# A four-layer cross-attention kernel: one engine meeting taken out between two layers, and the order of issue changed in two earlier places

## The chip, the cores and the metric

The kernel runs on one core of a Trainium2 chip. The time is device microseconds (us) of one launch. The engines are TensorE (PE, matmuls; its weight loads are PEld), VectorE (DVE), ScalarE (ACT), GpSimd (POOL) and SyncE (SP, which here only issues DMAs). Every engine runs its own program in order, and programs wait for each other on semaphores.

## The reference, cut to what matters

Four layers follow one another over `x`, 4 batches of 256 tokens with 256 channels:

```
L0: x = x + tanh(gate) * (softmax(q k^T / 4, masked) v) Wo     16 heads of 16; k, v from layernorm(ctx)
L1: an RWKV block (recurrent scan and channel mixing)
L2: x = layernorm(x + (softmax(q k^T * s + mask) v) Wo + bo)   32 query heads of 8 on 8 key/value heads
L3: twice:  x = x + cross_attention(layernorm(x), ctx)         16 heads of 128, and one extra bias key/value
    then    x = x + gelu(layernorm(x) W1 + b1) W2 + b2
```

All softmaxes subtract the row maximum. The keys and values of L3 come from `ctx` alone, so they are projected early, in the shadow of the layers before.

## The kernel before, in words

There are five stages, written one after the other: `stacked_first` (L0), `rwkv_block` (L1), `stacked_attention` (L2), `wide_stream` (the two attentions of L3) and `mlp`. Between stages the four compute engines meet (`meet`, L294): each drains, signals `arrived`, and waits until SP (`lead`, L300) has cleared all stage semaphores and set each engine's `go`.

**L0 and L2** work in steps (8 each; a step is half of a batch's heads) of 8 slots. In `at`, the number of a slot, negative slots are a run-up. For every head PE first makes the plain scores of a step (`fill`, L636 and L1338), DVE takes row maxima of them, POOL splits these into three bf16 parts, PE turns them (`flip_maxima`), ACT copies the row to SBUF and issues a DMA on its own queue that lays it beside the queries (`fetch_maxima`, L841 and L1541; semaphores `max0_landed`, `max_landed`). Then `transposed_scores` (L648, L1353) gives scores with the maximum already subtracted, ACT takes exponents, `weigh` multiplies by the values. Operands of a step are three-part bf16 rows: they are written to DRAM (`keep_keys0`, `keep_queries0`; `keep_key_parts`, `keep_query_parts`) and read back spread over the partitions (`spread0`, L542: eight DMAs for one step; `spread_rows`, L1238: three DMAs for one batch). SP issues all of these in one written order (`stacked0_sp`, L583; `stacked_sp`, L1291). In L0, `spread0(m)` must have landed before `fill(m, 0)` in slot 8(m-2); step 5 is spread in slot 18, behind `keep_queries0(3)` in slot 17:

```
605:                if prepared(n - 1) is not None and i == 1:
606:                    keep_queries0(sp, prepared(n - 1))
607:                if 1 <= n <= STEPS0 - 4 and i == 2:
608:                    spread0(sp, n + 3)
```

**Units ahead.** The 128 matmul groups that project `ctx` to L3's keys and values (`project_ahead`, L1101: 4 matmuls of 512 columns) are strewn over the slots. The first eight, from a quarter of a value matrix, belong to L0: `first_unit(0)` stands in the opening (L723), the other seven at `FIRST_AT` (L516). In the opening PE turns x and the normalised context of batch 1 (`flip_x(1)`, `flip_a(1)`) and projects keys and queries of batch 1 (L720 to L728); `flip_a(1)` stands behind `first_unit(0)`, which waits for two loads.

**L2's end** (`finish`, L1508): last `weigh`, first query projection of L3 (`project_head`), `flip_od`, DVE `normalise`, `flip_on`, second `project_head`, `project_out` into J1, and `bias_rows_pe` (32 matmuls into bank S0) with ACT's copy of its result to `v17`. SP has meanwhile loaded keys and values of group 0 of L3 in four pieces (`load_kept(sp, 0, 0)`, L1322), issued when the last unit is stored. Then the meeting.

**L3's stream** handles 128 items (8 groups of 16 heads). For item n: `logits(n)` on PE (two matmuls; it waits for its piece in `kept_landed`, for a bias column in `kept_bias`), DVE `maxima`, ACT `exponents`, DVE `divide`, PE `turn`, ACT copy, PE `weigh`, DVE copy, PE `add_head`; `project_query` runs two items ahead. `logits(0)` stands at the start of the stage (L2575), and DVE adds L2's last output to x (L2711, L2713) before `maxima(0)`.

Of the kernel before, what the change touches and what calls it, by code (L numbers as in the profile page):

```python
# [62 lines left out]
def build(nc, d, out):  # L63
    with ExitStack() as ctx:
# [216 lines left out]

        def stage_names():
# [233 lines left out]
        FIRST_AT = [-15, -13, -9, -8, -6, -5, -3]  # L516
# [66 lines left out]
        def stacked0_sp(sp, load_first, load_rest, load_values):  # L583
# [14 lines left out]
            for at in range(-LEAD0, LAST0):  # L598
# [9 lines left out]
                if 1 <= n <= STEPS0 - 4 and i == 2:  # L608
                    spread0(sp, n + 3)
# [5 lines left out]
        def stacked_first():  # L615

            def pe_program(pe):
# [102 lines left out]
                flip_x(1, J0)  # L720
                pe.wait_ge(loaded["ctxT"], 16)
                pe.wait_ge(loaded["quarter"], 16)
                first_unit(0)  # L723
                flip_a(1, O1)
# [3 lines left out]
                queries(1, T1)  # L728
                for at in range(-LEAD0, LAST0):
# [61 lines left out]
                    if at in FIRST_AT:  # L791
                        first_unit(1 + FIRST_AT.index(at))
# [7 lines left out]
            def act_program(act):  # L800
# [69 lines left out]
                fetch_queries(1, T1)  # L870
                act.wait_ge(loaded["const"], 16 * 2)
                act.activation(gate[:, 1:2], gate[:, 0:1], ACT.Tanh).then_inc(gate_ready, 1)
                act.wait_ge(mask_ready, 4)
                for at in range(-LEAD0, LAST0):
                    n, i = at // CHUNKS0, at % CHUNKS0
                    if at - 1 in FIRST_AT:
                        u = 1 + FIRST_AT.index(at - 1)
                        copy_first(act, (J1, O0)[u % 2], u)
# [412 lines left out]
        def stacked_sp(sp, load_wide, load_ahead):  # L1291

            for at in range(IN_TAIL, LAST):
                n, i = at // CHUNKS2, at % CHUNKS2
                b = n // 2
                if i == 0 and n % 2 == 0 and n >= 0 and b + 1 < B:
                    if b > 0:
                        sp.wait_ge(st_done, 4 * b * CHUNKS2)
                    else:
                        sp.wait_ge(filled, SLOTS2 + 1)  # L1300
                    spread_rows(sp, b + 1)
# [7 lines left out]
                if at == 6:  # L1309
                    sp.wait_ge(tail_done, 4)  # L1310
                    load_ahead("k")
# [22 lines left out]
        def stacked_attention():  # L1334
            chunk_order = [(kt, j, gp) for kt in range(TQ) for j in range(2) for gp in range(2)]

            def pe_slots(pe):
# [170 lines left out]
                def finish():  # L1508
# [6 lines left out]
                    flip_od(STEPS2 - 1, T0)  # L1515
                    flip_on(STEPS2 - 1, T1)
                    project_head(pe, 0, 1, 1)
                    project_out(B - 1, J1)
                    bias_rows_pe(pe, 0, S0)
# [7 lines left out]
            def pe_program(pe):  # L1527
                slot, finish = pe_slots(pe)[0:2]
                for at in range(IN_TAIL, LAST):
                    slot(at)  # L1530
                finish()
                meet(pe, "pe")

            def act_slots(act):
# [51 lines left out]
                def finish():  # L1586
# [5 lines left out]
                    bias_rows_act(act, 0, S0)  # L1592
# [7 lines left out]
            def act_program(act):  # L1600
# [4 lines left out]
                meet(act, "act")  # L1605

            def pool_program(pool):
# [49 lines left out]
                meet(pool, "pool")  # L1657
# [109 lines left out]
            def dve_program(dve):  # L1767
# [4 lines left out]
                meet(dve, "dve")  # L1772
# [681 lines left out]
        def load_layer1(split_k):  # L2454
# [22 lines left out]
            "last2_read", "last2_var", "last2_rstd", "last2_normed", "last2_step", "last2_scaled"))  # L2477
        FRONT_AT = 8
        ROWS_AT = 3 * HEADS3 + 12

        def stream_sp(sp, load_wide):

            for n in "qo":
                load_wide(1, n)
# [6 lines left out]
        def wide_stream():  # L2491
# [9 lines left out]
            def pe_program(pe):  # L2501
                def logits(n):
                    g, a, h = of(n)
                    if n >= AHEAD:
# [9 lines left out]
                    mm.then_inc(logits3_done, 1)  # L2514

# [26 lines left out]
                def weigh(n):  # L2542
                    g, a, h = of(n)
                    pe.wait_ge(pt3_ready, n + 1)
                    for st in range(TQ):
# [29 lines left out]
                logits(0)  # L2575
# [65 lines left out]
            def pool_program(pool):  # L2641
                pool.memset(weight_blocks[:, :, :, 16:17], 1.0)
                pool.memset(weight_blocks[:, :, :, 17:32], 0.0)
                for keys, _ in kept:
                    pool.tensor_copy(keys[:, :, S], head_cols("bias_k1")).then_inc(kept_bias, 1)
# [26 lines left out]
            def dve_program(dve):  # L2672
# [193 lines left out]
        def _(sp):  # L2866
# [64 lines left out]
            for i in range(len(programs["pe"]) - 1):  # L2931
# [114 lines left out]
```

## Time and profile before

| | |
|---|---|
| median of 3 runs | 1253.01 us (1250.61 to 1253.26) |
| profiled execution | 1252.52 us; its span 1250.7 us |
| PE busy | 1188.3 us, 95% of the span |
| DVE, ACT, POOL busy | 63%, 43%, 17% |
| granted TensorE clock, mean | 0.984 |

The span is what the trace covers; 1.8 us of the profiled execution lie around it. A granted clock of 1.00 is 2.4 GHz and of 0.50 is 1.2 GHz. Times in the rows are counted from the span's start. The chain that ended last is PE in 86% of the span, so the places of interest are those in which PE stands still or runs at 0.50.

### The profile page before, as it was taken

To read this page: it belongs to the slowest core of one execution; us is meant where nothing else is said; L and a number is where in the kernel's file an instruction comes from. 1 tells how busy PE (TensorE), PEld (TensorE's weight loads), DVE (VectorE), ACT (ScalarE), POOL (GpSimd) and SP (SyncE) were. 2 spreads that over 40 slices of the span, in tenths; PEclk is the share of its full clock that TensorE was granted. 3 is DMA by queue.
4 is the path that set the end of the run, shared out by engine and by line. 5 is a ranking of instruction groups with operands and counts; after the bars stand their busy time and mean duration, and the time that the engine had idled before them with its cause. 6 is when DMAs were issued, how large, how long until landed. Compare 5 with 4: busy or idle time off the path is not lost.

```text
span 1250.7 us, 17685 instructions
## 1 busy us (share of the span) xinstructions
PE 1188.3 (95%) x5936; PEld 837.6 (67%) x5936; DVE 792.5 (63%) x2357; ACT 537.4 (43%) x1233; POOL 216.0 (17%) x430
## 2 busy tenths in 40 slices
PE   6899899999998799999998999999999999999998
PEld 4466554655555344444335888888888888888887
DVE  4655377868685577878754666666656676666530
ACT  2365533445445245455553434343434334343432
POOL 2240152434244101120111000000000000000000
PEclk8998999999999799999999999999999999999999
DMA  8659032021116635154249230302112120500000
GB/s 245 161 159 280 9 129 85 34 76 43 68 48 197 189 144 166 73 164 144 78 146 322 97 130 6 114 23 97 39 55 80 37 99 21 182 1 2 1 9 26
DMA packets 95033, 124.42 MB, mean 99 GB/s; under 512 B 7264, under 2 KB 72960, under 8 KB 92704
## 3 DMA queue, kind: packets, MB, share of 16 engines
q1 hardware_dynamic: 94320, 123.00, 30.4%
q8 instruction: 48, 0.79, 0.3%
q10 hardware_dynamic: 624, 0.30, 0.1%
q14 instruction: 41, 0.34, 0.1%
HBM read 79.33 MB, written 43.65 MB: 98 GB/s over the span
## 4 chain that ended last, share of the span: by engine, by line
PE 86%; DVE 3%; ACT 3%; issue 2%; POOL 2%; DMA 2%; SPq 1%; ACTq 1%; POOLq 0%; DVEq 0%
PE J L2538 9%; PE TT L2546 9%; PE J L2558 9%; PE OO L1112 5%; PE OO L1109 5%; PE TT L2522 5%; PE S L2512 4%; PE OO L2512 4%; PE J L1112 3%; PE J L1376 2%; PE J L323 2%; PE J L1109 2%; PE OO L2779 2%; PE S L1348 2%; PE J L332 2%
## 5 line engine op out<-in xcount | busy, mean ns | idle before, releaser
L2616 ACT ACTIVATE PT<-TT 128x512 f32<-128x512 f32 x128 | 76.4, 597 | 282.4 <-PE TT L2522 282.4
L2651 POOL COPY On<-probs 128x8 f32<-128x8 f32 x128 | 29.2, 228 | 471.3 <-DVE probs L2686 442.1
L2697 DVE TENSOR_SCALAR QK<-J,cols 128x256 f32<-128x256 f32 x126 | 60.9, 484 | 70.3 <-PE J L2538 70.3
L2686 DVE TENSOR_SCALAR probs<-probs,inv 128x257 f32<-128x257 f32 x256 | 79.0, 351 | 4.5
L2522 PE MATMUL TT<-ident,probs 128*128 128x128 f32 x512 | 77.3, 274 | 2.6 <-DVE probs L2686 2.6
L1112 PE MATMUL OO<-ctxT,weights_a 128*128 128x512 f32 x144 | 70.2, 610 | 5.8 <-SPq L307 3.3
L2522 PEld LDWEIGHTS TT<-ident,probs 128*128 128x128 f32 x512 | 64.1, 141 | 16.3 <-DVE probs L2686 3.4
L2692 DVE COPY km<-TT 128x256 f32<-128x256 f32 x128 | 54.2, 423 | 30.8 <-PE TT L2546 30.5
L1109 PE MATMUL OO<-weights_a,ctxT 128*128 128x512 f32 x136 | 69.3, 634 | 3.4 <-SPq L307 2.9
L2402 DVE TENSOR_TENSOR_SCAN early<-km,early 128x256 f32<-128x256 f32 x64 | 64.3, 1044 | 10.9 <-ACT early L2160 10.1
L2546 PE MATMUL TT<-PT,weights_a 128*128 128x256 f32 x256 | 66.2, 381 | 0.0
L2558 PE MATMUL J<-early,km 128*128 128x256 f32 x256 | 65.8, 379 | 0.3 <-DVE km L2692 0.3
L2546 PE MATMUL TT<-PT,early 128*128 128x256 f32 x256 | 65.9, 380 | 0.0
L2558 PE MATMUL J<-weights_a,km 128*128 128x256 f32 x256 | 65.6, 379 | 0.0
L2678 DVE TENSOR_REDUCE maxes<-OO 128x1 f32<-128x257 f32 x128 | 48.5, 420 | 26.0 <-PE OO L2512 25.0
L2678 DVE TENSOR_REDUCE maxes<-S 128x1 f32<-128x257 f32 x128 | 48.4, 420 | 24.8 <-PE S L2512 24.8
L2608 ACT ACTIVATE probs<-S,maxes 128x257 f32<-128x257 f32 x128 | 59.4, 474 | 3.5 <-DVE maxes L2678 3.5
L2608 ACT ACTIVATE probs<-OO,maxes 128x257 f32<-128x257 f32 x128 | 59.3, 473 | 0.1
L2546 PEld LDWEIGHTS TT<-PT,weights_a 128*128 128x128 f32 x256 | 49.2, 192 | 6.9
L2546 PEld LDWEIGHTS TT<-PT,early 128*128 128x128 f32 x256 | 48.5, 190 | 7.0 <-ACT PT L2616 0.4
L2558 PEld LDWEIGHTS J<-early,km 128*128 128x128 f32 x256 | 48.3, 190 | 7.1 <-DVE km L2692 0.5
L2558 PEld LDWEIGHTS J<-weights_a,km 128*128 128x128 f32 x256 | 48.5, 190 | 6.7
(423 smaller groups left out, 2624.2 us busy)
## 6 DMA issues: line engine op xcount, KB each, us to landing
wide_keys<-weights_a SPq DMA_DIRECT2D x43, 256.0 KB, 2.1
wide_values<-weights_a SPq DMA_DIRECT2D x40, 256.0 KB, 2.0
weights_a<-wide_keys SPq DMA_DIRECT2D x16, 512.0 KB, 7.3
weights_a<-wide_values SPq DMA_DIRECT2D x16, 512.0 KB, 8.5
early<-wide_keys SPq DMA_DIRECT2D x16, 512.0 KB, 8.1
early<-wide_values SPq DMA_DIRECT2D x16, 512.0 KB, 9.0
query_parts<-weights_a SPq DMA_DIRECT2D x32, 192.0 KB, 2.7
weights_a<-in_L_xattn_wv SPq DMA_DIRECT2D x2, 2048.0 KB, 8.8
```

The lines of the kernel that those rows point to most:

```text
L1109: mm = pe.matmul(bank_[:, :], ctxT[:, k, b * S + t * P:b * S + (t + 1) * P], values_, start=(k == 0), stop=(k == KC - 1))
L1112: mm = pe.matmul(bank_[:, :], ahead_k[a][:, k, h * P:(h + 1) * P], ctxT[:, k, pair * 512:pair * 512 + 512], start=(k == 0), stop=(k == KC ...
L2402: ins = dve.tensor_tensor_scan(state[j % 2][:, half, 1:S + 1], wT[:, half, :], kv[j % 2][:, half, :], start[:, half, j:j + 1], ALU.mult, A ...
L2512: mm = pe.matmul(L_[n % 2][qt][:, 0:T], QK[:, n % 2, 0, qt * P:(qt + 1) * P], kept[g % 2][0][:, h, :], start=True, stop=True)
L2522: mm = pe.transpose(T0[:, st * S + qt * P:st * S + (qt + 1) * P], P_[n % 2][:, qt, st * P:(st + 1) * P], ident[:, :])
L2538: mm = pe.matmul(J0[:, 0:S], wide[a][0][:, k, h * P:(h + 1) * P], hidden[g % 2][:, k, :], start=(k == 0), stop=(k == KC - 1))
L2546: mm = pe.matmul(T1[:, 0:S], kept[g % 2][1][:, st, h * P:(h + 1) * P], PT[:, n % 2, st * S:(st + 1) * S], start=(st == 0), stop=(st == TQ ...
L2558: pe.matmul(J1[:, qt * S:(qt + 1) * S], avT[:, n % 2, qt * P:(qt + 1) * P], wide[a][1][:, h, :], start=(h == 0 and qt == 0), stop=False)
L2608: ins = act.activation(P_[n % 2][:, qt, 0:T], L_[n % 2][qt][:, 0:T], ACT.Exp, bias=maxes[:, qt, n % 32:n % 32 + 1], accum_out=sums[:, qt, ...
L2616: act.activation(PT[:, n % 2, :], T0[:, :], ACT.Copy).then_inc(pt3_ready, 1)
L2678: ins = dve.tensor_reduce(maxes[:, qt, n % 32:n % 32 + 1], L_[n % 2][qt][:, 0:T], AX_X, ALU.max, negate=True)
L2686: ins = dve.tensor_scalar(P_[n % 2][:, qt, :], P_[n % 2][:, qt, :], inv[:, qt, n % 32:n % 32 + 1], None, ALU.mult)
```

## The change: what it does

Five edits, in order of time.

1. **Opening of L0.** `flip_a(1, O1)` stands ahead of the waits for `ctxT` and `quarter`, so ahead of `first_unit(0)`. `first_unit(1)` stands behind `queries(1, T1)`; six units instead of seven are left for `FIRST_AT`, in other slots. ACT's copies follow.
2. **L0, SP.** `spread0(5)` is issued in slot 16 instead of 18, so ahead of `keep_queries0(3)`.
3. **L2, SP.** The spread of batch 1 waits until the first row of maxima has landed (`max_landed`).
4. **L2, SP, slot 6.** Three more waits, and one instruction that clears the 40 semaphores that stages share by name.
5. **L2 to L3.** No engine meets any more. `logits(0)` is issued between `flip_od` and `flip_on` of L2's end. The bias rows go to bank T1 and wait for `ot2_ready`. The first DVE work of L3 is `maxima(0)` and `divide(0)`; the two additions follow. POOL, SP and PE get single waits in place of the meeting.

```diff
-        FIRST_AT = [-15, -13, -9, -8, -6, -5, -3]
+        FIRST_AT = [-14, -12, -9, -7, -5, -3]
...
-                if 1 <= n <= STEPS0 - 4 and i == 2:
+                if 1 <= n <= STEPS0 - 4 and i == (0 if n == 2 else 2):
                     spread0(sp, n + 3)
...
                 flip_x(1, J0)
+                flip_a(1, O1)
                 pe.wait_ge(loaded["ctxT"], 16)
                 pe.wait_ge(loaded["quarter"], 16)
                 first_unit(0)
-                flip_a(1, O1)
                 pe.wait_ge(keys0_ready, 1)
                 keys(1, T0)
                 pe.wait_ge(queries0_ready, 1)
                 queries(1, T1)
+                first_unit(1)
...
                     else:
                         sp.wait_ge(filled, SLOTS2 + 1)
+                        sp.wait_ge(max_landed, 16)
                     spread_rows(sp, b + 1)
...
                 if at == 6:
                     sp.wait_ge(tail_done, 4)
+                    sp.wait_ge(st_done, 1)
+                    sp.wait_ge(sum_ready, 1)
+                    sp.wait_ge(weighed_ready, 1)
+                    clear_stage(sp, 40)
                     load_ahead("k")
...
                     flip_od(STEPS2 - 1, T0)
+                    logits = slots3["pe"](pe)
+                    logits(0)
                     flip_on(STEPS2 - 1, T1)
                     project_head(pe, 0, 1, 1)
                     project_out(B - 1, J1)
-                    bias_rows_pe(pe, 0, S0)
+                    pe.wait_ge(ot2_ready, STEPS2)
+                    bias_rows_pe(pe, 0, T1)
...
-                meet(pe, "pe")
...
         def stream_sp(sp, load_wide):
 
+            sp.wait_ge(av2_done, 4 * STEPS2)
+            sp.wait_ge(sum_ready, 2 * LAST)
+            sp.wait_ge(max_taken, STEPS2 * SLOTS2)
+            sp.wait_ge(max_landed, 16 * STEPS2)
+            sp.wait_ge(out2_done, B)
             for n in "qo":
                 load_wide(1, n)
...
                 def logits(n):
                     g, a, h = of(n)
+                    if n < AHEAD:
+                        pe.wait_ge(q_ready, n + 1)
+                    if n == 1:
+                        pe.wait_ge(ahead_copied, 2 * UNITS)
...
             def pool_program(pool):
+                pool.wait_ge(av2_done, 4 * STEPS2)
+                pool.wait_ge(ahead_done, 2 * UNITS)
+                pool.tensor_copy(kept[0][0][:, :, S], head_cols("bias_k1")).then_inc(kept_bias, 1)
+                pool.wait_ge(on2_flipped, STEPS2)
                 pool.memset(weight_blocks[:, :, :, 16:17], 1.0)
                 pool.memset(weight_blocks[:, :, :, 17:32], 0.0)
-                for keys, _ in kept:
-                    pool.tensor_copy(keys[:, :, S], head_cols("bias_k1")).then_inc(kept_bias, 1)
+                pool.wait_ge(out2_done, B)
+                pool.tensor_copy(kept[1][0][:, :, S], head_cols("bias_k1")).then_inc(kept_bias, 1)
...
+                maxima(0)
+                divide(0)
+                dve.wait_ge(out2_done, B)
                 dve.tensor_tensor(xn[:, :, :], two(J1), x_of(B - 1), ALU.add).then_inc(last2_read, 1)
                 dve.wait_ge(last2_read, 1)
                 chain.link(dve.tensor_tensor(xn[:, :, :], xn[:, :, :], bo2, ALU.add))
-                maxima(0)
-                divide(0)
...
                 elif i == 2:
                     stacked_sp(sp, load_wide, load_ahead)
-                    lead(sp, 1)
```

The first `weigh` of L3 also waits for `v17_ready`, since it writes bank T1. `copy_first(act, (J1, O0)[1], 1)` stands behind ACT's `fetch_queries(1, T1)`.

## Rows read from the trace of the kernel before

**Rows 1.** Waits on PE: waiting line and releaser; us in total, times, longest
```profile
PE TT L1363 <- DMA weights_a<-early: 4.9, 1, 4.9
```

**Rows 2.** Timeline of the opening: start us, us, engine, line, operands; idle before it
```profile
19.53 0.73 DVE L264 TENSOR_SCALAR xn<-weights_a,moments,rstd 128x256 f32<-128x256 f32 x2 [0.28 <-POOL rstd L271]
20.30 3.75 PE L1109 MATMUL J<-early,ctxT 128*128 128x512 f32 x4 [3.74 <-DMA early<-in_L_xattn_wv]
...
26.11 3.68 PE L323 MATMUL TT<-V,early 128*128 128x256 f32 x8 [1.20 <-ACT V L812]
...
29.63 1.89 PE L323 MATMUL TT<-hT,early 128*128 128x256 f32 x8
```

**Rows 3.** Windows: stretch, length, busy PE PEld DVE ACT POOL, granted clock, DMA
```profile
20.30:29.40 9.10, 7.89 (x16) 4.69 (x17) 1.42 (x4) 1.51 (x3) 0.00 (x0) 0.50 0.72 166
422.10:439.00 16.90, 11.41 (x23) 3.95 (x23) 6.03 (x29) 3.54 (x4) 0.00 (x0) 0.50 0.51 154
674.70:678.00 3.30, 3.30 (x11) 2.73 (x12) 1.10 (x5) 1.51 (x5) 0.07 (x1) 0.50 1.01 421
```

**Rows 4.** Timeline of SP's issues in L0, from 80 us on
```profile
80.85 1.87 SPq L2868 DMA_DIRECT2D early<-in_state  x1
...
86.75 0.90 SPq L539 DMA_DIRECT2D query_parts<-weights_a  x2
...
92.12 0.58 SPq L571 DMA_DIRECT2D km<-query_parts  x1
```

**Rows 5.** Timeline of PE in L0: slots 24, 32 and 48, and step 5's fill
```profile
91.30 0.60 PE L657 MATMUL TT<-early,weights_a 128*128 128x256 bf16 x4
95.97 0.39 PE L643 MATMUL S<-weights_a,km 128*128 128x256 bf16 x1 [4.07 <-DMA km<-query_parts]
...
108.56 0.60 PE L657 MATMUL OO<-km,weights_a 128*128 128x256 bf16 x4
...
129.65 0.60 PE L657 MATMUL TT<-early,weights_a 128*128 128x256 bf16 x4
```

**Rows 6.** Timeline of L2's first slots: spreads, maxima row, a unit, slots 0 and 3
```profile
418.45 0.84 SPq L1245 DMA_DIRECT2D km<-query_parts  x2
...
422.09 0.76 ACTq L1547 DMA_DIRECT2D weights_a<-early  x1
...
424.36 3.78 PE L1109 MATMUL OO<-weights_a,ctxT 128*128 128x512 f32 x4
...
433.08 1.01 PE L1363 MATMUL TT<-weights_a,early 75*128 75x512 bf16 x2 [4.93 <-DMA weights_a<-early]
...
444.74 0.60 PE L1363 MATMUL TT<-weights_a,early 75*128 75x512 bf16 x2
```

**Rows 7.** DMA queues from 426 to 434 us: queue, packets, MB, share
```profile
q10 hardware_dynamic: 51, 0.02, 1.5%
```

**Rows 8.** Line L1161 between 660 and 661.9 us: the first piece's values
```profile
L1161 SPq DMA_DIRECT2D weights_a<-wide_values x1: 508/508/508, 660.9 to 660.9; - x1
...
DMA to landing us min/median/max: 5.1/5.1/5.1
```

**Rows 9.** Timeline from L2's end to the first items of L3
```profile
663.78 0.44 PE L1398 MATMUL TT<-ident,On 128*128 128x128 f32 x2 [0.91 <-DVE On L1707]
...
666.96 1.93 PE L446 MATMUL S<-weights_a,mask_b 128*32 128x256 f32 x32
669.02 0.38 ACT L452 ACTIVATE KT<-S 128x256 f32<-128x256 f32 x1 [4.38 <-PE S L446]
...
670.63 1.10 PE L2512 MATMUL S<-weights_a,QK 128*128 128x257 f32 x4 [1.73 <-POOL early L2645]
670.74 0.69 DVE L2713 TENSOR_TENSOR xn<-xn,rows 128x512 f32<-128x512 f32 x1
...
674.57 1.03 PE L2522 MATMUL TT<-ident,probs 128*128 128x128 f32 x4 [1.97 <-DVE probs L2686]
...
679.34 0.60 PE L2522 MATMUL TT<-ident,probs 128*128 128x128 f32 x4
```

More of the change, by code:

```diff
@@ L280, in build, with clear_stage @@
         shared = []
+        def clear_stage(sp, count):
+            numbers = [s.num for s in shared[:count]]
+            assert numbers == list(range(numbers[0], numbers[0] + count))
+            sp.sem_clear(range(numbers[0], numbers[0] + count))
         def stage_names():
@@ L791, in pe_program @@
                     if at in FIRST_AT:
-                        first_unit(1 + FIRST_AT.index(at))
+                        first_unit(2 + FIRST_AT.index(at))
                 weigh(STEPS0 - 1, 1)
@@ L870, in act_program @@
                 fetch_queries(1, T1)
+                copy_first(act, (J1, O0)[1], 1)
                 act.wait_ge(loaded["const"], 16 * 2)
@@ L876, in act_program @@
                     if at - 1 in FIRST_AT:
-                        u = 1 + FIRST_AT.index(at - 1)
+                        u = 2 + FIRST_AT.index(at - 1)
                         copy_first(act, (J1, O0)[u % 2], u)
@@ L1591, in finish @@
                     act.wait_ge(ahead_stored[2], stores_before(2 * UNITS, 2))
-                    bias_rows_act(act, 0, S0)
+                    bias_rows_act(act, 0, T1)
                 def second_batch():
@@ L1604, in act_program @@
                 finish()
-                meet(act, "act")
             def pool_program(pool):
@@ L1656, in pool_program @@
                 bias_rows_pool(pool, 0)
-                meet(pool, "pool")
             def dve_slots(dve):
@@ L1771, in dve_program @@
                 finish()
-                meet(dve, "dve")
             slots2.update(pe=pe_slots, act=act_slots, dve=dve_slots)
@@ L2477, in build @@
             "last2_read", "last2_var", "last2_rstd", "last2_normed", "last2_step", "last2_scaled"))
+        slots3 = {}
         FRONT_AT = 8
@@ L2499, in of, with first_logits @@
                 return n // HEADS3, n // HEADS3 // B, n % HEADS3
-            def pe_program(pe):
+            def first_logits(pe):
                 def logits(n):
                     g, a, h = of(n)
+                    if n < AHEAD:
+                        pe.wait_ge(q_ready, n + 1)
+                    if n == 1:
+                        pe.wait_ge(ahead_copied, 2 * UNITS)
                     if n >= AHEAD:
@@ L2514, in logits, with pe_program @@
                     mm.then_inc(logits3_done, 1)
+                return logits
+            slots3["pe"] = first_logits
+            def pe_program(pe):
+                logits = first_logits(pe)
                 def turn(n):
@@ L2544, in weigh @@
                     pe.wait_ge(pt3_ready, n + 1)
+                    if n == 0:
+                        pe.wait_ge(v17_ready, 1)
                     for st in range(TQ):
@@ L2573, in add_bias_rows @@
                     mm.then_inc(out3_done, 1)
-                logits(0)
                 for n in range(ITEMS3):
```

## The prediction

> **What bounds the kernel now.** First the page: PE is busy in nearly all of the span, so a reordering can only win where PE stands still or runs at its lower clock. Then the waits of PE, the longest single ones: `transposed_scores` in L2 waits 4.9 us for a DMA that ACT issued [rows 1], and `fill` of step 5 in L0 waits 4.07 us for a spread [rows 5]. Then the timelines around these two, the opening and the layer change, with the windows for the clock. Each standstill is followed by work at 1.2 GHz: the windows behind the opening's wait, around the wait in L2 and at the start of L3 have a granted clock of 0.50 [rows 3]. So a wait costs itself plus half of the slow work behind it. The change touches four places. All sums are made against the profiled execution (span 1250.7, time 1252.5 us); the median of the runs, 1253.0, is 0.5 us above it.
>
> **Place A, the opening.** Before, PE stands until the quarter matrix lands at 20.3, does `first_unit(0)` (3.75 us, at 1.2 GHz), then `flip_a(1)`; only then can ACT fetch it, and `keys(1)` waits 1.20 us for that [rows 2]. After, `flip_a(1)` needs the centred context, which DVE ends at 20.26, and the four transposes run as the matrix lands. PE then does the unit while ACT fetches, so the 1.20 us go. Nothing is added: the same transposes, units and copies, in another order. `first_unit(1)` moves from between the first fills to ahead of them; before and after it PE would have stood waiting for DVE's split of the queries there, which hides it. If this cover were gone, it would cost one unit, about 1.9 us. There is a second part: keys and queries run from 26.11 to 31.52, 5.4 us, for two equal projections of which one costs 1.89 us at full clock [rows 2], and the low clock ends at about 29.4 [rows 3]. Without the gap PE works in one piece from 20.3 and may be granted 2.4 GHz some us earlier; all of it would be worth 5.4 - 3.8 = 1.6 us. The later waits move with it, since ACT, DVE, POOL and SP are released by these projections. Bounds: 0.5 (the units between the fills delay the maxima) to 4.0 (a later slow stretch goes too). I take 1.2 + 1.2 = **2.4 us**.
>
> **Place B, step 5's spread.** In slot 24 PE is at 91.30 and waits until 95.97 for rows whose last DMA SP issued at 92.12; it landed 3.85 us after its issue [rows 4, 5]. These eight issues stand behind `keep_queries0(3)` at 86.75, which itself waited for POOL's split. From the end of that (87.65) to the start of the last issue are 4.5 us. After, the spread is ahead of it, behind the loads of slot 14 and 15, whose last issue ends at 80.85 + 1.87 = 82.7 [rows 4]. Its own condition, step 1's scores, is met by then: they end with slot 15, eight slots of 10.55 us in all ahead of 91.30, so at about 80.7. So the last issue starts at about 82.8 + 4.5 = 87.3 and lands at 91.1, just ahead of PE's 91.3 plus one group. What it is moved past on SP: two issues of `keep_queries0(3)` start 5 us later than they might, about 88, and land by 91; four loads of L1's weights stand behind them, and `spread0(6)`, which needs that landing and has until slot 32. The price of B is read from slots: slots 24 to 31 take 108.56 - 91.30 = 17.26 us, and slots 32 to 47 take 129.65 - 108.56 = 21.09, 10.55 for eight with a fill and the same odd jobs [rows 5]. So B is worth 17.26 - 10.55 = **6.7 us**, wait and slow clock together. Bounds: 3 (rows land 2 us after PE is there, and the clock falls again) to 6.7.
>
> **Place C, the spread in L2.** The row of maxima of step 0 is issued at 422.09 and PE gets it at 433.08 [rows 6]. Between 426 and 434 its 51 packets trickle through [rows 7] among those of batch 1's spread, issued at 418.45 and before [rows 6]. After, SP waits for the row, so ahead of it in the DMA engines are only a weight load, which lands by 424.36 (the unit that needs it starts then), and one store. The row should then land by 426 to 427.5; PE reaches slot 0 at 424.36 + 3.78 = 428.14, so the 4.93 us wait goes. The clock is low from 422.1 to 439.0 [rows 3]; with PE working in one piece from 424.36 it should rise earlier. At most half of 433.08 to 439.0, 2.95 us, is won there, 7.9 in all; a rise 2 us after 428.14 costs 1.1. I take **6.8 us**. Behind SP's new wait stand the three spread issues and then the store of the first unit of L2. PE needs the spread in slot 3, where it is now at 444.74 [rows 6], after at about 438; the spread took until 433 from the first row packet at 426, so issued at 427 it has two thirds (keys and first half of queries, all that slot 3 needs) by about 434. Some 4 us of room. Bounds: 1 to 7.9.
>
> The Trainium skill, "DMA: Bandwidth & Descriptors", section "Queues, rings and completion order", says that each DMA engine takes turns between the queues that have work, a packet at a time. By it a small DMA on ACT's queue need not wait for SP's spread to finish, and the new wait would win little. The trace has the turns, one row packet now and then over some 7 us, but the row still ended only with the spread. By the rule the sum would lose most of C, and this is the first rival below.
>
> The three further waits and the clearing in slot 6 stand on SP ahead of a load that is needed 26 slots later: nothing.
>
> **Place D, the layer change.** Before, from the bias rows' end at 668.9 to `logits(0)` at 670.63 PE stands 1.73 us, then 1.97 us until `turn(0)` at 674.57 [rows 9], and works at 1.2 GHz from 674.7 to 678.0 [rows 3]. After, `logits(0)` stands ahead of `flip_on`. It needs the first query (DVE, just behind `normalise`, which `flip_on` waits for until 663.78), and the first piece of keys and values: its second DMA is issued at 660.9 and lands 5.1 us later, at **666.0** [rows 8]. PE is free at 662.9 (0.91 us ahead of `flip_on`), so it stands 3.1 us, with `flip_on`, the query, the output projection and the bias rows queued behind. `logits(0)` 1.1 us, to 667.1; then what took 668.9 - 663.78 = 5.1 us before, to 672.2; ACT's copy for `v17`, 0.4 and a wake-up, stands ahead of `exponents(0)`, which so starts at 672.65 (the maxima are long there). Before, the time from the end of `logits(0)` to `turn(0)` was 674.57 - 671.73 = 2.84 for maxima, exponents and divide; the last two are about 1.9. So `turn(0)` comes at 674.55: nothing is won, the meeting's 1.7 us went into the wait for the piece. The two additions of 0.69 us now stand between `divide(0)` and `maxima(1)`; `turn(1)` comes at 674.55 + 1.4 + 2.84 = 678.8 against 679.34, 0.5 earlier, of which the statistics behind `divide(1)` take about 0.2. Against that, a standstill of 3.1 us is longer than the 1.97 us that preceded the slow stretch of 674.7 to 678.0, so I expect one such stretch in the projections: half of 3.3 us, 1.6, less the 0.3. I take **-1.0 us** after allowing that the old slow stretch may not come back. Bounds: -3 (two stretches) to +3 (piece there at once). POOL's bias column, which waits for the last `weigh`, and PE's guards for banks are covered by the same 3.1 us; SP's new waits end with `out2_done`, at about 670, as the meeting did.
>
> **Sum.** 2.4 + 6.7 + 6.8 - 1.0 = 14.9 us; 1252.5 - 14.9 = **1237.6 us**.
>
> **Rivals.**
> *The row is late for another reason.* If the weight load, the store and the fabric delay the row as the spread did, C keeps 1 to 3 us: about 1242.5. For: the row's packets do take turns with others [rows 7]. Against: nothing else is issued ahead of it after 418. Chance 0.13.
> *Step 5 still waits.* The margin in B is a few tenths; a spread that lands 2 us late leaves 3 us of B: 1241.3. Chance 0.09.
> *The layer change pays.* If the piece is there, `turn(0)` comes 2 us earlier and the slow stretch goes: +3 in place of -1, 1233.6. Against: rows 8. Chance 0.09.
> *Slower.* The stream of L3 starts with DVE behind, and its loop (copy, maxima, exponents, divide of one item, some 3.3 us with the copy) becomes the bound of all 128 items, which now take about 3.9 us on PE. It decides from 14.9 / 128 = 0.12 us per item; at 0.2 the time is 1263. Against: 3.3 us is under 3.9, so a backlog of 1.4 us should melt in a few items. Chance 0.03.
> *Nothing comes of it.* Every won wait is waited again at the next row or meeting: 1252.5. Chance 0.03.
>
> **How the numbers follow.** My forecast has 0.63. A difference under 0.2%, 2.5 us, can't be told from none here. Faster: 0.63 + 0.13 + 0.09 + 0.09 = 0.94; same 0.03; slower 0.03. The forecast's own terms move by about 1.5 (A), 1.2 (C's clock) and 2 (D), so 1234 to 1241; the first two rivals reach 1243, the third 1233.6, all partly. 1231.5 to 1244 leaves out under 2 in 10.
>
> **What would show it.** A: no wait of `keys(1)` for ACT's V; slot 0 of L0 about 2.4 us earlier. B: slots 24 to 31 take about 10.6 us and `fill` waits for no DMA. C: no wait on ACT's row, slot 3 some 6.8 us nearer to the first unit. D: PE waits about 3 us at `logits(0)` for a DMA into `weights_a`, and `turn(0)` keeps its distance from the last `weigh`. The prediction is wrong if the waits of rows 1 and 5 are there again, or if items of L3 take more than 3.9 us.

## The result and the profile after

The changed kernel took 1239.05 us in the median (1236.86 to 1240.31, 4 runs), the kernel before beside it 1252.64 (1250.61 to 1253.26): ratio 0.9896, 95% interval 0.9878 to 0.9914. The forecast was 1237.6. The profiled execution has a span of 1237.5 us, 13.2 less than before. Below, A to C are three changes of order (the opening, step 5's spread in L0, the spread in L2), and D is the layer change.

The first view is the windows of the changed kernel (stretch, length, busy time of PE, PEld, DVE, ACT and POOL, granted clock, DMA share, GB/s), as in [rows 3].

```profile
18.80:25.50 6.70, 5.55 (x11) 3.24 (x12) 2.27 (x7) 1.62 (x3) 0.25 (x1) 0.50 0.60 174
36.30:39.80 3.50, 2.85 (x12) 1.32 (x11) 2.81 (x17) 0.60 (x1) 0.00 (x0) 1.00 0.72 186
94.40:101.20 6.80, 5.53 (x49) 3.96 (x48) 3.42 (x16) 3.05 (x6) 1.43 (x7) 1.00 1.05 341
411.30:421.50 10.20, 9.48 (x27) 3.81 (x26) 6.83 (x35) 2.23 (x3) 0.28 (x2) 0.50 0.74 248
650.30:653.60 3.30, 3.13 (x9) 2.51 (x10) 0.00 (x0) 0.38 (x1) 0.24 (x2) 0.50 1.08 366
1175.90:1179.20 3.30, 3.30 (x9) 2.59 (x9) 2.43 (x9) 1.03 (x1) 0.69 (x1) 0.50 0.00 0
```

The four stretches at 0.50 are all that this profile has from 18 us on, 23.9 us; before there were 41.0 us of them. The one that stood behind the first fills is gone, and so is the one behind slot 24. That of L2 is 10.2 us long instead of 17.1. A new one stands at 1175.9, in the MLP, which the change does not touch.

**Place A**, PE's timeline of the opening (start, duration, engine, line, operands, idle time before it), and slot 0 of L0, of the changed kernel first and of the kernel before under it:

```profile
19.95 1.11 PE L321 MATMUL OO<-ident,xn 128*128 128x128 f32 x4 [3.75 <-DVE xn L264]
20.86 3.62 PE L1117 MATMUL J<-early,ctxT 128*128 128x512 f32 x4
24.27 2.54 PE L329 MATMUL TT<-V,early 128*128 128x256 f32 x8
26.65 1.89 PE L329 MATMUL TT<-hT,early 128*128 128x256 f32 x8
...
48.77 0.60 PE L663 MATMUL TT<-km,weights_a 128*128 128x256 bf16 x4 [0.45 <-ACT early L1138]
```

```profile
53.66 0.60 PE L657 MATMUL TT<-km,weights_a 128*128 128x256 bf16 x4 [0.48 <-ACT early L1130]
```

`flip_a(1)` stands first and `keys(1)` (L329) waits for nothing; in [rows 2] it waited 1.20 us. The standstill ahead of both is as long as it was, 3.75 us, now for DVE instead of the quarter matrix. Queries of batch 1 end at 28.54 instead of 31.52, and slot 0 comes at 48.77 instead of 53.66: 4.9 us.

**Place B**, slots 24, 32 and 40 of L0 on PE's timeline, against [rows 5], and behind it the issues around the row of maxima of step 4 on the timeline of all engines:

```profile
86.41 0.60 PE L663 MATMUL TT<-early,weights_a 128*128 128x256 bf16 x4
...
98.38 0.61 PE L663 MATMUL OO<-km,weights_a 128*128 128x256 bf16 x4 [1.27 <-DMA km<-weights_a]
...
110.53 0.61 PE L663 MATMUL TT<-km,weights_a 128*128 128x256 bf16 x4 [1.44 <-DMA km<-weights_a]
```

```profile
89.84 0.58 SPq L577 DMA_DIRECT2D early<-query_parts  x1
90.30 0.73 ACTq L854 DMA_DIRECT2D km<-weights_a  x1
90.52 0.40 SPq L2903 DMA_DIRECT2D weights_a<-in_L_xattn_wv  x1
```

The wait of `fill` for the spread is gone. In its place slots 32 and 40 wait for rows of maxima, the DMAs that ACT issues. Slots 24 to 47 take 121.08 - 86.41 = 34.7 us, where 38.3 stood before and three times 10.55 was forecast. The row of step 4 goes out at 90.30, 0.2 us ahead of the 2 MB value load, and is needed 6.7 us later, at 86.41 + 10.55 = 96.96.

**Place C**, PE in L2 (the unit, slot 0 and slot 3), against [rows 6]:

```profile
415.84 3.76 PE L1117 MATMUL OO<-weights_a,ctxT 128*128 128x512 f32 x4
419.38 1.06 PE L1376 MATMUL TT<-weights_a,early 75*128 75x512 bf16 x2
...
429.18 0.60 PE L1376 MATMUL TT<-weights_a,early 75*128 75x512 bf16 x2
```

Slot 0 follows the unit without a wait, and slot 3 comes 13.3 us after the start of the unit, before 20.4: 7.0 us.

**Place D**, the layer change, against [rows 9]: the first `project_head`, `logits(0)`, ACT's copy and exponents, the first and the third `turn`; then the landing of the piece's values, issued at 645.30; then the first `project_head` and the third `turn` of the kernel before:

```profile
645.73 1.13 PE L428 MATMUL J<-hT,weights_a 128*128 128x256 f32 x4
...
650.47 2.05 PE L2534 MATMUL S<-weights_a,QK 128*128 128x257 f32 x4 [3.18 <-issue]
...
657.93 0.38 ACT L458 ACTIVATE KT<-TT 128x256 f32<-128x256 f32 x1 [4.57 <-PE TT L452]
658.21 0.47 ACT L2638 ACTIVATE probs<-S,maxes 128x257 f32<-128x257 f32 x1
...
660.14 0.66 PE L2551 MATMUL TT<-ident,probs 128*128 128x128 f32 x4 [1.27 <-DVE probs L2720]
...
668.33 0.61 PE L2551 MATMUL TT<-ident,probs 128*128 128x128 f32 x4
```

```profile
DMA to landing us min/median/max: 5.1/5.1/5.1
```

```profile
661.31 1.13 PE L422 MATMUL J<-hT,weights_a 128*128 128x256 f32 x4
...
683.23 0.60 PE L2522 MATMUL TT<-ident,probs 128*128 128x128 f32 x4
```

`logits(0)` (L2534) waits 3.18 us, and the profile names no releaser. The query was ready at 648.54 and POOL's bias column at 646.10. What is left is the first piece, whose values landed at 650.4, 5.1 us after their issue, as in [rows 8]. `turn(0)` comes 14.41 us after L2's end begins its first `project_head` ("the head" below), before 13.26; the third `turn` comes after 22.60, before 21.92, which is 0.7 us lost.

The pair of traces thus shows A 4.9, B 3.7, C 7.0, D -0.7, and -1.7 for the stretch in the MLP (half of its 3.4 us): 13.2 us.

### The profile page after: what moved, and what is told of

Same layout as the page of the kernel before. It is cut to its first block, busy times and chain, and to the rows that moved or that the text cites. A ratio compares the mean times of both kernels' runs of the same rounds, so it can differ in the third digit from the quotient of the medians.

```text
span 1237.5 us, 17677 instructions
## 1 busy us (share of the span) xinstructions
PE 1183.3 (96%) x5936; PEld 835.9 (68%) x5936; DVE 792.6 (64%) x2357; ACT 536.9 (43%) x1233; POOL 215.6 (17%) x430
## 4 chain that ended last, share of the span: by engine, by line
PE 87%; DVE 4%; ACT 3%; issue 2%; POOL 2%; DMA 2%; ACTq 1%; SPq 0%; POOLq 0%; DVEq 0%
PE J L2589 9%; PE J L2567 9%; PE TT L2577 9%; PE OO L1117 5%; PE OO L1120 5%; PE S L2534 5%; PE TT L2551 5%; PE OO L2534 4%; PE J L1120 3%; PE J L1389 2%; PE J L329 2%; PE OO L2814 2%; PE S L1361 2%; PE J L1117 2%; PE TT L329 2%
## 5 line engine op out<-in xcount | busy, mean ns | idle before, releaser
L2414 DVE TENSOR_TENSOR_SCAN early<-km,early 128x256 f32<-128x256 f32 x64 | 64.3, 1045 | 10.9 <-ACT early L2172 10.1
L2712 DVE TENSOR_REDUCE maxes<-S 128x1 f32<-128x257 f32 x128 | 48.4, 420 | 24.2 <-PE S L2534 24.2
```

The lines of the kernel that those rows point to most:

```text
L2414: ins = dve.tensor_tensor_scan(state[j % 2][:, half, 1:S + 1], wT[:, half, :], kv[j % 2][:, half, :], start[:, half, j:j + 1], ALU.mult, A ...
L2712: ins = dve.tensor_reduce(maxes[:, qt, n % 32:n % 32 + 1], L_[n % 2][qt][:, 0:T], AX_X, ALU.max, negate=True)
```

## How the runs are compared

The clock's stretches turned out to stand elsewhere in other executions of the same program. So each time is also split into a **fixed part**, the span times its mean granted clock, and the rest, which the clock takes (a standstill in a slow stretch is counted in the rest too, and the clock of an execution is listed to 0.001, which is 0.6 us either way, so the split of one execution is rough). Differences are of means over executions, with 95% intervals by Welch's method. The kernel before, in 57 further executions: mean 1248.1 us (1243.3 to 1255.9), fixed part 1232.1, clock 14.2. In three sets of these beside the other kernels its mean was 1248.6, 1247.6 and 1248.1, so sets can be compared to about 1 us. The profile on which the prediction rests lost 20.5 us to the clock, and all four executions of the first set took more than 1250.6 us, as only 15 of the 57 did; whether that was chance is open. Time and the clock's part have a correlation of 0.94 over these executions. The changed kernel, in 12: mean 1238.9 (1236.9 to 1241.3), fixed 1225.6, clock 11.5. So the change is worth 9.2 us on average (7.9 to 10.5), 6.5 of it in the fixed part; in the first set it was 13.6.

**The changed kernel again.**

> The changed kernel itself, beside the kernel before. The profiles so far show that stretches at a granted clock of 0.50 come in other places in each execution: the kernel with the old opening had none in its opening, the changed kernel had one. Theory: an execution's time is a fixed part (span times mean granted clock: 1230.2 us for the profile of before, 1225.5 for the changed kernel) and a part that the clock takes (20.5 and 12.0 us), and the second varies by several us between executions of one program. Then this kernel has 1225 to 1226.5 us of the first part, times between 1234 and 1243, and is 9 to 13 us faster than before in one set of executions. Rival: the times of 1236.9 to 1240.3 are what the program takes and the slow stretches belong to its places: all executions within 1.5 us of 1239, and the profile has the same four stretches.

Median 1238.20 (1237.36 to 1241.30), ratio 0.9925 (0.9897 to 0.9952), fixed part 1225.6, as the theory says. Its profile has slow stretches at 20.0, 33.6, 142.9, 415.9 and 651.5 us, and none in the MLP. The places vary, as the theory says, but the times less than it says, and the gain over the kernel before beside it, 8.3 us between the medians, is under its 9 to 13. These two windows are of this execution; the second is twice as long as at the same place above.

```profile
20.00:23.40 3.40, 2.81 (x7) 1.78 (x8) 1.99 (x6) 1.02 (x2) 0.00 (x0) 0.50 0.65 170
651.50:658.20 6.70, 5.96 (x15) 4.80 (x16) 1.15 (x3) 0.38 (x1) 0.24 (x2) 0.50 1.07 367
```

## Undoing one part at a time

**The opening.** (Shown in part; the slots of the units and ACT's copies go back with it.)

```diff
                 flip_x(1, J0)
-                flip_a(1, O1)
...
                 first_unit(0)
+                flip_a(1, O1)
...
                 queries(1, T1)
-                first_unit(1)
```

> The changed kernel with the opening as it was: flip_a(1) behind first_unit(0), first_unit(1) in slot -15 again, seven units in the slots. Theory: the opening is worth 4.9 us in the profiled pair, of which 2.6 us come through keys and queries (the wait for ACT's V and the earlier clock), 1.6 us because no slow stretch follows the first fills, and 0.4 is a later start of the program. So this kernel takes about 1239.0 + 4.5 = 1243.5 us, slot 0 comes at 53 to 54 us again instead of 48.8, and a stretch at 0.50 lies somewhere between 36 and 40 us. Rival 1, the slow stretch is a matter of where the standstill falls and not of the order: slot 0 at 51.5 to 52.5 and the time about 1241.5. Rival 2, something later takes the gain: under 1240.

Median 1237.88 (1233.37 to 1245.65), ratio 0.9928 (0.9897 to 0.9958): no slower than the changed kernel, so rival 2 by its number. The trace says why, and it is none of the three. PE's first two rows and the window:

```profile
19.37 1.96 PE L1115 MATMUL J<-early,ctxT 128*128 128x512 f32 x4 [1.81 <-DMA early<-in_L_xattn_wv]
...
23.11 1.97 PE L329 MATMUL TT<-V,early 128*128 128x256 f32 x8 [1.20 <-ACT V L818]
```

```profile
19.30:29.50 10.20, 6.61 (x28) 4.40 (x29) 4.48 (x12) 3.77 (x8) 3.78 (x4) 1.00 0.89 197
```

The wait for ACT's V is back, but PE stood only 1.81 us for the quarter matrix, the clock stayed at 1.00, and slot 0 came at 47.47, ahead of the changed kernel's 48.77. The standstill was short at both ends: the quarter matrix was there at 19.37 instead of 20.30, and PE's work ahead of it ended at 17.56 instead of 16.56. A second set of executions of the same kernel:

> The changed kernel with the old opening once more. So far its mean time is that of the changed kernel (1238.8 and 1239.0 us), though its fixed part is 1.7 us longer; single times lie between 1233.4 and 1245.7. Theory: the opening saves the wait for ACT's V, 1.2 to 1.7 us, in every execution, and whether the first 40 us have 0, 3.4, 6.8 or 13.7 us at a granted clock of 0.50 is settled in each execution by how long PE stands for the quarter matrix (1.81 us with none, 3.74 with 13.65); so the fixed part is 1227 to 1228 again, and the profile has either a standstill under 2 us and no slow stretch before 40 us, or one above 3 and several. Rival: the old opening has no price in the fixed part; then it is 1225.6 here.

Median 1240.64 (1235.41 to 1246.40), ratio 0.9942 (0.9917 to 0.9967), fixed part 1226.8, just under the 1227 to 1228 of the theory. The profile shows the other of the theory's two cases:

```profile
20.21 3.75 PE L1115 MATMUL J<-early,ctxT 128*128 128x512 f32 x4 [3.74 <-DMA early<-in_L_xattn_wv]
```

```profile
19.30:29.50 10.20, 8.08 (x16) 4.92 (x17) 2.19 (x6) 1.51 (x3) 0.02 (x1) 0.50 0.72 158
```

A second stretch follows at 36.4 to 39.8, as before the change. With the old opening four profiles thus show, before 41 us, a standstill of 3.74 us and 13.65 us at 0.50 (two of them), or 1.8 to 2.0 us and none. With the new one all nine show 3.69 to 3.76 us, and 3.4 or 6.8 us at 0.50. The new order saves 1.4 us of the fixed part (0.1 to 2.8) and replaces a gamble by its middle; in time it is worth 0.9 us (-1.0 to 2.8), which these executions cannot tell from nothing.

**Step 5's spread.**

```diff
-                if 1 <= n <= STEPS0 - 4 and i == (0 if n == 2 else 2):
+                if 1 <= n <= STEPS0 - 4 and i == 2:
```

> The changed kernel with spread0(5) in slot 18 again, behind keep_queries0(3). Theory: the wait of fill in slot 24 of about 4 us and the slow clock behind it are there again (6.7 us in slots 24 to 31), but the waits for the rows of maxima of steps 4 and 5 (1.27 and 1.44 us, with slots 24 to 39 taking 3.0 us more than 10.55 for eight) go, because the row of step 4 then has the standstill to land in; so this kernel is about 3.7 us slower than the changed one: 1242.7 us. Rival, the waits for the rows come from elsewhere (the faster opening, the loads) and stay: 6.7 us slower, 1245.7 us, with both waits in the trace.

Median 1244.01 (1241.79 to 1245.38), ratio 0.9960 (0.9943 to 0.9978), 5.0 us above the changed kernel (3.9 to 6.1), 3.0 of them in the fixed part: between the theory's number and the rival's. PE's rows, and the window behind the first:

```profile
91.40 0.61 PE L649 MATMUL S<-weights_a,km 128*128 128x256 bf16 x2 [4.34 <-DMA km<-query_parts]
...
104.98 0.61 PE L663 MATMUL OO<-km,weights_a 128*128 128x256 bf16 x4 [1.10 <-DMA km<-weights_a]
```

```profile
89.40:96.10 6.70, 4.70 (x29) 2.34 (x30) 2.12 (x9) 1.28 (x2) 0.00 (x0) 0.50 0.92 195
```

The fill waits again and the clock falls; slot 32 still waits 1.10 for its row, slot 40 only 0.19. So 5.6 us of waits stand against 2.7 in the changed kernel, close to the 3.0 of the fixed part. What the edit wins beyond that exchange is this clock: behind the waits for rows that it leaves, up to 1.8 us each, no profile here has a slow stretch.

**SP's wait for the row.**

```diff
                         sp.wait_ge(filled, SLOTS2 + 1)
-                        sp.wait_ge(max_landed, 16)
```

> The changed kernel without SP's wait for the first row of maxima ahead of the spread of batch 1. Theory: transposed_scores of slot 0 waits some 4 to 5 us for the row again, and the distance from the unit ahead of it to slot 3 is about 20 us instead of 13.3; the fixed part (span times granted clock) grows by about 4 to 5 us, the time by 5 to 7: about 1245. Rival: the row comes in time because SP reaches the spread at another moment than before; no wait in slot 0, time 1239.

Median 1245.52 (1243.89 to 1247.80), ratio 0.9985 (0.9965 to 1.0004), 6.8 us above the changed kernel (5.5 to 8.0), fixed part 4.4 above.

```profile
417.99 3.10 PE L1117 MATMUL OO<-weights_a,ctxT 128*128 128x512 f32 x4
425.93 1.01 PE L1375 MATMUL TT<-weights_a,early 75*128 75x512 bf16 x2 [4.83 <-DMA weights_a<-early]
```

The old wait is there, slot 3 comes 19.0 us after the unit, and the row's 51 packets start 5.0 us after its issue (421.0 against 416.05), where with the wait they start after 1.7 (415.6 against 413.89). The theory holds. By the rule of turns that the prediction took from the Trainium skill ("DMA: Bandwidth & Descriptors", "Queues, rings and completion order") the wait should have won little; here the measurement decides against it. Turns are seen only from 421.0 on, some three row packets every half microsecond; the 5.0 us ahead of the first packet are not among them.

**The layer change.** The kernel before with the first three edits only; edits 4 and 5, the whole layer change, are left out. Shown in part, against the changed kernel:

```diff
                     flip_od(STEPS2 - 1, T0)
-                    logits(0)
                     flip_on(STEPS2 - 1, T1)
...
+                meet(pe, "pe")
...
+                logits(0)
                 for n in range(ITEMS3):
```

> The kernel before with the three earlier edits (opening, spread0(5), the wait for the row) and the old layer change: meeting, logits(0) behind it, bias rows in S0. Theory: the layer change itself gains nothing. From project_head to the third turn it takes 22.09 us in the profile of before and 22.60 us in that of the changed kernel, so this one is 0.5 us faster than the changed kernel, about 1238.5. Rival: the slow stretches made the layer change of the changed kernel look worse than it is; then this one is 1 to 2 us slower than the changed kernel, about 1240.5.

Median 1238.69 (1235.77 to 1240.82), ratio 0.9925 (0.9896 to 0.9953), against the changed kernel 0.5 us less (-2.4 to 1.3), as the theory says; of the rival's 1 to 2 us more, the interval leaves the lower end. PE's timeline and the window of the whole change:

```profile
653.58 1.10 PE L2515 MATMUL S<-weights_a,QK 128*128 128x257 f32 x4 [1.73 <-POOL early L2648]
...
657.52 0.66 PE L2525 MATMUL TT<-ident,probs 128*128 128x128 f32 x4 [1.96 <-DVE probs L2689]
```

```profile
640.00:665.00 25.00, 19.66 (x124) 12.80 (x123) 11.35 (x34) 8.63 (x22) 1.85 (x8) 1.00 0.89 313
```

`turn(0)` comes 13.26 us after the head, which begins at 644.26, to the hundredth as in the profile of before, and the third turn after 20.54, there 21.92: only the slow stretch behind `turn(0)` is missing. In the seven profiles with `logits(0)` ahead of `flip_on`, `turn(0)` comes after 14.2 to 16.0 us, always with 3.4 or 6.8 us at 0.50. In time the edit makes no difference that can be measured; in the timeline the third turn comes after 22.4 to 24.2 us, 1.8 to 3.6 later than with the meeting and no slow stretch.

## Three things that the traces suggested

**The loads of L0 behind the rows.**

```diff
+                if n == 4 and i == 6:
+                    sp.wait_ge(max0_landed, 16 * 6)
...
                     sp.wait_ge(query0_kept, 16 * 2 * B)
+                    sp.wait_ge(max0_landed, 16 * 5)
                     load_values()
```

> The changed kernel, with SP's 2 MB value load and the weight loads behind it held until the row of maxima of step 4 has landed, and the weight loads of step 4 until the row of step 5 has. Theory, the rows stand among these loads in the DMA engines: row 4, issued at 90.3, lands by 94.5 instead of 98.2, both waits in slots 32 and 40 go, slots 24 to 39 take about 21.1 us instead of 24.1, and the time falls by about 3.0 us to 1236.0. Rival 1, row 4 stands behind the spread that ends being issued at 90.4, not behind the loads: the wait in slot 32 stays, that of slot 40 may go, gain 0.5 to 1.5 us. Rival 2, the held loads make the start of L1 late: slower than 1239.

Median 1237.98 (1235.45 to 1241.02), ratio 0.9919 (0.9891 to 0.9948), 1.0 us below the changed kernel (-3.1 to 1.1), where the theory had 3: the time decides nothing. The trace does. SP's and ACT's issues, PE's only wait for a DMA in slots 24 to 47, and the packets of ACT's queue (q10; packets, MB, share of the engines' time), first of this kernel from 90.4 to 92.3, then of the changed one from 90.3 to 97.9:

```profile
90.40 0.73 ACTq L857 DMA_DIRECT2D km<-weights_a  x1
93.18 0.40 SPq L2906 DMA_DIRECT2D weights_a<-in_L_xattn_wv  x1
```

```profile
108.38 0.61 PE L666 MATMUL TT<-km,weights_a 128*128 128x256 bf16 x4 [0.64 <-DMA km<-weights_a]
```

```profile
q10 hardware_dynamic: 27, 0.01, 4.1%
```

```profile
q10 hardware_dynamic: 27, 0.01, 0.6%
```

The row of step 4 ends its packets at 92.3, 1.9 us after its issue, instead of 97.8, 7.5 us after it. The spread ahead of it is the same in both, so rival 1 falls: what held the row was a load issued 0.2 us behind it. Profiles of other kernels here bear this out. With the row between 0.1 us behind the load and 0.2 ahead of it, it took 7.1 to 7.7 us to its last packet (five profiles). With 0.6 ahead it took 2.8 and 3.9 us, and slot 32 did not wait (two profiles: the old opening's second, and the one with `logits(0)` behind the output projection). Slots 24 to 47 take 32.4 us. The row of step 5 still comes late by 0.64 us. It went out at 100.94, when the value load had just landed (100.89), but its packets start only at 106.9: the spread of step 7 stands ahead of it, and behind the value load this spread's last DMA took 7.9 us to land, 3.9 in the version below in which the value load comes later. That the time shows so little has a reason in the other profiles: with the L0 of the changed kernel the two waits come to 2.7, 2.7, 2.6 and 3.1 us in four profiles and to 0.2 in a fifth, that of the next kernel, so part of the gain is there by chance without the edit.

**`logits(0)` behind the output projection.**

```diff
                     flip_od(STEPS2 - 1, T0)
-                    logits(0)
                     flip_on(STEPS2 - 1, T1)
                     project_head(pe, 0, 1, 1)
                     project_out(B - 1, J1)
+                    logits(0)
```

> The changed kernel, with logits(0) issued behind project_out instead of between flip_od and flip_on. Theory: the 3.2 us that PE stands for the first piece of keys are filled with flip_on, the query and the output projection, the piece has landed (650.4) when logits(0) is issued at about 651.3, the slow stretch at 650 to 654 goes, and turn(0) comes at about 656.9 instead of 660.1, held by ACT's copy of the bias rows' result ahead of exponents(0): 3.2 us faster, about 1235.9 us. Rival 1: DVE's additions, which then are free earlier, and the loop's own start take it back: 0 to 1 us. Rival 2: the time moves by a slow stretch at the start of the MLP or elsewhere that comes or goes, 1.7 us either way.

Median 1235.49 (1232.55 to 1237.53), ratio 0.9897 (0.9869 to 0.9924), 3.5 us below the changed kernel (-5.3 to -1.7), as the theory says.

```profile
651.13 1.03 PE L2534 MATMUL S<-weights_a,QK 128*128 128x257 f32 x4
...
656.35 0.66 PE L2551 MATMUL TT<-ident,probs 128*128 128x128 f32 x4 [1.27 <-DVE probs L2720]
```

`logits(0)` waits for nothing, the clock is 1.00 from 640 to 665, and `turn(0)` comes 10.79 us after the head, which begins at 645.56.

**All three together**, and with them the value load behind the last row of all, and ACT's copy of the bias rows' result behind `exponents(0)` instead of ahead of it.

```diff
+                if n in (3, 4) and i == 6:
+                    sp.wait_ge(max0_landed, 16 * (n + 2))
...
-                if n == 3 and i == 4:
+                if n == 6 and i == 7:
...
+                    sp.wait_ge(max0_landed, 16 * STEPS0)
                     load_values()
...
                 exponents(0)
+                bias_rows_act(act, 0, T1)
```

> The changed kernel with three things more: the rows of maxima of steps 4 and 5 ahead of the loads, with the 2 MB value load behind the last row; logits(0) behind project_out; ACT's copy of the bias rows' result behind exponents(0). Theory: no wait for a row in slots 32 and 40 (2.7 us less), turn(0) 9.3 us behind project_head instead of 14.4 (3.2 us by the order of logits(0) and 1.6 by ACT's copy), so the fixed part falls by about 5.5 us to 1220 and the time to about 1233. Rival 1: the late value load is waited for at the start of L1, between 143 and 155 us: 3 to 6 us lost there. Rival 2: the row of step 5 still waits about 0.6 us, as it stands behind its own spread.

Median 1229.91 (1228.90 to 1232.04), ratio 0.9854 (0.9822 to 0.9886); once more:

> The kernel with the three additions once more, beside the other two on one chip. Theory: 1229 to 1231 us, fixed part 1220.5, some 16 to 18 us under the kernel before and 8 under the changed one. Rival: its times of 1228.9 to 1232.0 had a good draw of the clock; then it comes to 1232 to 1235.

Median 1229.67 (1228.95 to 1229.89), ratio 0.9862 (0.9837 to 0.9887), fixed part 1220.4. This is the fastest version, 9.0 us below the changed kernel (7.9 to 10.1) over both sets. In the first profile, slots 24 and 48 of L0 and the rows at the layer change:

```profile
86.50 0.60 PE L666 MATMUL TT<-early,weights_a 128*128 128x256 bf16 x4
...
118.12 1.04 PE L666 MATMUL TT<-early,weights_a 128*128 128x256 bf16 x8
...
645.67 0.44 PE L1414 MATMUL TT<-ident,On 128*128 128x128 f32 x2 [0.91 <-DVE On L1721]
...
648.75 1.03 PE L2535 MATMUL S<-weights_a,QK 128*128 128x257 f32 x4
...
652.55 0.66 PE L2552 MATMUL TT<-ident,probs 128*128 128x128 f32 x4
```

`turn(0)` comes 9.36 us after the head, which begins at 643.19 (9.3 expected), and waits for nothing. No row is waited for in L0; slots 24 to 47 take 118.12 - 86.50 = 31.62 us, three times 10.54. Its row of step 5, at 100.93 behind the same spread, ended its packets at 103.4. Both rivals fall: L1 starts without a wait for the late load.

> The kernel with the three additions (rows ahead of the loads, logits(0) behind project_out, ACT's copy later), and the old opening. Theory: the fixed part is 1.7 us longer than with the new opening, 1222.1 against 1220.5, and the time, with the clock's part as it falls, 1229 to 1235. Rival: with no waits for rows behind it, the opening's 1.2 us count in full with the clock: 3 to 5 us slower than 1230.

With the old opening besides: median 1232.41 (1226.72 to 1235.68), ratio 0.9886 (0.9856 to 0.9915), fixed part 1221.9, 1.5 above that with the new one (0.6 to 2.4), near the 1.7 expected; the rival's 3 to 5 us in time are neither shown nor excluded (1.6, -2.1 to 5.3). The profiled execution, 1224.9 us, is the shortest span of all: its standstill was 1.97 us and its opening kept 1.00.

## Why the prediction came out as it did

The time was right, 1237.6 against 1239.05, and 1238.9 over 12 executions. The gain was not: 14.9 us forecast, 9.2 measured. That the time came out is luck in good part, as two errors stood against each other. The sum starts from one execution of 1252.5 us, 4.4 above the mean of 57, which lost 6.3 us more than that mean to the clock; and two terms were too large.

| Place | forecast | pair of traces | by undoing it (95%) |
|---|---|---|---|
| A, opening | 2.4 | 4.9 | 0.9 (-1.0 to 2.8) |
| B, step 5 | 6.7 | 3.7 | 5.0 (3.9 to 6.1) |
| C, row in L2 | 6.8 | 7.0 | 6.8 (5.5 to 8.0) |
| D, layer change | -1.0 | -0.7 | -0.5 (-2.4 to 1.3) |

The last column sums to 12.2, not 9.2; each of its entries holds the same uncertain mean of the changed kernel, so they err together, and this difference of 3 us is left open.

*The premise* "each standstill is followed by work at 1.2 GHz" does not hold in the prediction's own profile: the 1.93 us ahead of the MLP and the waits of 1.4 to 2.0 us between 154 and 398 us were followed by none.

*A.* The wait of 1.20 us went, as the step says, and the fixed part has it (1.4). "May be granted 2.4 GHz some us earlier", 1.2 us in the sum, was the step that failed: it takes the slow stretches of [rows 3] as a property of the order. They belong to a standstill whose length changes from one execution to the next, 1.8 or 3.7 us, and the new order made PE stand 3.7 us in all nine profiles, as `flip_a(1)` then waits for DVE. The same step read from the pair alone would have been called too low by half.

*B.* The spread arrives in time, as worked out. The failed step is the price "read from slots": that slots 32 to 47 keep 10.55 for eight. That held before by 1.3 us: the row of step 4 went out at 101.91, 2.25 us behind the value load, ended its packets 5.4 us later and was needed after 6.65. In the changed kernel it went out 0.2 us ahead of the load and took 7.5 us, with 6.7 to the need. The undone edit shows how thin the old margin was: there the row of step 4 is late by 1.10, in the old order of SP. The question "what is late next" was asked for the spreads on SP and not for the rows on ACT. With the rows' way cleared, slots 24 to 47 take 31.62 against 38.35: 6.7 us, the forecast number.

*C* was right in mechanism and size, clock included. *D* was right in its mechanism: the standstill at `logits(0)` (3.1 forecast, 3.18), nothing won by the missing meeting, one slow stretch (one or two). With that stretch `turn(0)` came 1.2 us later than before, and the forecast, which counts the stretch by itself, has 1.3. The forecast did not ask whether the order could be better; behind the output projection the same instruction costs nothing.

*Rivals.* The row in L2 and step 5's spread were in time. The loop of L3 is not DVE's: an item takes 4.018 us on average, group ends included, in every profile of every kernel here, the one before too. So the prediction's sign of being wrong, more than 3.9 us an item, was set on an item inside a group (683.23 - 679.34 = 3.89 before) and is met by the kernel before as well. The standstill at `logits(0)` excludes that the layer change pays as it stands. That every won wait is waited again came true in part, at B: 2.7 us of the 4.07 came back at the next two rows.

## What to carry to other kernels

Before a gain is read from one profile, split the time into span times granted clock and the rest, and look at a second execution: here one program spread over 12 us, nearly all of it clock. When a wait is taken out, list every DMA that lands in the time that the wait gave, on all queues, for the next wait is among them. A small transfer that the critical path needs should have landed before bulk on another queue is issued: here a lead of 0.2 us was worth nothing, and one of 0.6 us most of it.

## What the runs showed of the hardware

The same standstill is followed by a stretch at 1.2 GHz in one execution and by none in another. Ahead of the MLP PE stands 1.93 us in all thirteen profiles. Four of them then run its start at 0.50, and nine at 1.00. The first is the kernel before, the second the changed one, both PE's timeline:

```profile
1190.53 3.72 PE L323 MATMUL J<-hT,weights_a 128*128 128x256 f32 x16 [1.93 <-SPq L307]
```

```profile
1175.63 5.40 PE L329 MATMUL J<-hT,weights_a 128*128 128x256 f32 x16 [1.93 <-SPq L313]
```

Likewise the 2.53 us behind the first fills: of the changed kernel's two profiles, a slow stretch followed in one (at 33.6) and none in the other. After PE's first 15 us, each standstill of 3.13 us or more, in every profile, lay in a stretch at 0.50 or had one begin within 1.4 us behind it; the waits for rows in L0, up to 1.83 us, had none. The reverse does not hold: each of the thirteen profiles has 6.8 us or more at 0.50 around L2's first fills (in the changed one from 411.3), where PE's waits are many but none in the 12 us ahead of the stretch is over 0.8 us.

The other is the row: 12 KB on ACT's queue took 1.9 us to its last packet when nothing was issued behind it, and 7.5 us when 2 MB on SP's queue was issued 0.2 us later. Most of the delay lies ahead of the first packet, which came at 94.8, 4.5 us after the issue. The page of the Trainium skill named above has the engines alternate between queues packet by packet; what in that makes 27 packets take so long was not tried.
